# A decoder layer's running sums, kept token-major: the triangle of ones becomes the loaded operand, and the outputs are transposed instead of exp(-q)

## The reference, cut to what matters

```
qkv = _rms(x) @ w_qkv.T
q, k, v = jnp.split(qkv, 3, axis=-1)
q = _rms(q)
k = _rms(k)
w = jnp.exp(k)
kv_cum = jnp.cumsum(w * v, axis=1)
w_cum = jnp.cumsum(w, axis=1)
y = jax.nn.sigmoid(q) * (kv_cum / (w_cum + 1e-06))
uv = y @ w_swiglu.T
...
```

## Time and profile before

| | |
|---|---|
| median of three runs | 1407.77 us |
| the profiled execution | 1406.43 us |
| its span, first to last instruction | 1404.7 us |
| mean granted TensorE clock | 0.987 of full speed |
| TensorE busy with products over the span | 96% |
| VectorE, ScalarE, GpSimd busy | 58%, 43%, 37% |

### The profile page before, as it was taken

The page is one execution under the profiler, slowest core; times in us unless marked ns, Lnnn a source line. Parts: engine busy times, 40 slices in busy tenths (PEclk is TensorE's granted clock), DMA queues, the critical chain, the costliest instruction groups (busy, mean ns, idle before and its releaser), DMA issues.

```text
span 1404.7 us, 23677 instructions
## 1 busy us (share of the span) xinstructions
PE 1346.8 (96%) x8180; PEld 1072.4 (76%) x8180; DVE 819.7 (58%) x2085; ACT 607.9 (43%) x1135; POOL 515.2 (37%) x485
## 2 busy tenths in 40 slices
PE   8999999999999999999999999999988999999994
PEld 6788888888888888888877777777766887777662
DVE  5888765333333333333457787787776476666662
ACT  4444441111111111111127677777776223777772
POOL 4555442202020202020427654446453112565643
PEclk9999999999999999999999999999999899999997
DMA  6000012010010101010100000000011824465653
GB/s 255 1 0 0 0 42 94 0 45 26 21 45 1 45 0 45 0 46 0 49 27 2 20 21 20 21 20 3 5 47 59 351 86 157 85 110 93 106 97 45
DMA packets 20533, 73.41 MB, mean 52 GB/s; under 512 B 2320, under 2 KB 3344, under 8 KB 18000
## 3 DMA queue, kind: packets, MB, share of 16 engines
q0 software_dynamic: 10176, 25.17, 9.2%
q1 hardware_dynamic: 10256, 46.93, 9.0%
HBM read 52.95 MB, written 19.14 MB: 51 GB/s over the span
## 4 chain that ended last, share of the span: by engine, by line
PE 85%; DVE 6%; issue 3%; ACT 2%; DMA 2%; POOL 2%; DVEq 0%; POOLq 0%; ACTq 0%
PE ps L781 21%; PE ps L783 21%; PE ps L782 21%; PE ps L1029 6%; PE ps L1214 5%; PE ps L1021 2%; DVE den L1640 2%; PE ps L1053 2%; PE ps L1121 1%; PE ps L1018 1%; DMA h_rows<-hd 1%; PE ps L1047 1%; PE ps L1184 1%; POOL cols L673 1%; ACT cols L1434 1%
## 5 line engine op out<-in xcount | busy, mean ns | idle before, releaser
L781 PE MATMUL ps<-feat,wsplit 128*128 128x512 f32 (+1 forms) x672 | 247.2, 368 | 3.2 <-PE ps L783 2.2
L783 PE MATMUL ps<-feat,wsplit 128*128 128x512 f32 (+1 forms) x672 | 244.7, 364 | 0.0
L782 PE MATMUL ps<-feat,wsplit 128*128 128x512 f32 (+1 forms) x672 | 244.6, 364 | 0.0
L1291 ACT ACTIVATE sg<-ps 128x512 f32<-128x512 f32 x64 | 38.3, 598 | 368.8 <-PE ps L783 368.8
L1560 DVE TENSOR_TENSOR m_f<-ps,sg 128x512 f32<-128x512 f32 x64 | 44.2, 691 | 245.3 <-ACT sg L1291 245.3
L541 POOL CAST wsplit<-wraw 128x3072 fp32r<-128x3072 f32 x9 | 24.8, 2754 | 399.3 <-PEq L969 386.6
L1828 DVE CUSTOM_DVE_ANT_0 cols<-ps,msk 128x256 f32<-128x256 f32 (+1 forms) x512 | 146.1, 352 | 28.8 <-PE ps L1021 16.6
L781 PEld LDWEIGHTS ps<-feat,wsplit 128*128 128x128 f32 x672 | 126.7, 189 | 26.3 <-issue 6.6
L783 PEld LDWEIGHTS ps<-feat,wsplit 128*128 128x128 f32 x672 | 126.8, 189 | 20.1
L782 PEld LDWEIGHTS ps<-feat,wsplit 128*128 128x128 f32 x672 | 126.8, 189 | 19.6
L1422 ACT COPY cols<-ps 128x512 f32<-128x512 f32 x192 | 110.9, 578 | 61.2 <-PE ps L1029 61.2
(11 more groups left out here) (281 smaller groups left out, 3023.9 us busy)
## 6 DMA issues: line engine op xcount, KB each, us to landing
wraw<-weights SPq DMA_DIRECT2D x11, 1536.0 KB, 6.5
rawx<-weights SPq DMA_DIRECT2D x8, 1536.0 KB, 12.8
ctx_raw<-ctx_t SPq DMA_DIRECT2D x8, 512.0 KB, 4.6
h_rows<-hd POOLq DMA_DIRECT2D x16, 256.0 KB, 2.7
out<-acc SPq DMA_DIRECT2D x4, 1024.0 KB, 4.3
qkv_raw<-weights SPq DMA_DIRECT2D x6, 512.0 KB, 6.9
acc<-x SPq DMA_DIRECT2D x1, 3072.0 KB, 17.0
acc<-x SPq DMA_DIRECT2D x2, 512.0 KB, 6.8
```

The source lines that it names most:

```text
L781: nc.tensor.matmul(out_, w_hi, m_hi, start=first, stop=False)
L782: nc.tensor.matmul(out_, w_lo, m_hi, start=False, stop=False)
L783: return nc.tensor.matmul(out_, w_hi, m_lo, start=False, stop=last)
```

## The change

The two sides of the scan's products change places. `tri`'s two halves (triangle, and all ones) are now the loaded operand, and the data move through, 512 features at a time, tile by tile: tile 0 needs its own hi and lo for each of the two sums (4 products), tile 1 those of both tiles (8 products). The sums come out token-major, as `e_q` already lies, so exp(-q) is not transposed. ScalarE adds 1 to `e_q` in place (line 1329) and no longer copies w's sums; VectorE adds the 1e-6 where it added the 1. Tile t's output is transposed on TensorE (`turn_y`, lines 863 to 866) before its hi and lo go into `feat`, which are now read from PSUM. "Half 0" and "half 1" of the order become tile 0 and tile 1.

```diff
 (TensorE)
+            def scan(b, pb, tt):
+                if tt == 0:
                     pe.wait_ge(a["split"], 2 * b + 2)
-                    pe.wait_ge(a["e"], 2 * b + 2)
                 else:
-                    pe.wait_ge(a["y"], s)
+                    pe.wait_ge(a["y"], 2 * b + 1)
                 for bank, kind in ((5, 0), (4, 1)):
+                    terms = [(t, part) for t in range(tt + 1) for part in range(2)]
+                    for n, (t, part) in enumerate(terms):
+                        ones = tri[:, 0:P] if t == tt else tri[:, P:2 * P]
+                        mm = nc.tensor.matmul(ps[:, bank, :], ones, wv_s[:, place_a(pb, t), kind, part, :], start=(n == 0), stop=(n == len(terms) - 1))
+                mm.then_inc(a["scan"], 1)
+            def turn_y(b, tt):
+                pe.wait_ge(a["y"], 2 * b + tt + 1)
+                for k in range(KB):
+                    tr = nc.tensor.transpose(ps[:, 6, k * P:(k + 1) * P], den[:, k * P:(k + 1) * P], ident[:, :])
+                tr.then_inc(a["yT_ps"], 1)
...
                 project(b, 1, 0)
+                if not first:
+                    turn_y(b - 1, 0)
+                    scan(b - 1, 1 - pb, 1)
                 if not last:
                     transposes(b + 1, 0)
-                if not first:
-                    scan(b - 1, 1 - pb, 1)
                 project(b, 1, 1)
                 project(b, 1, 2)
+                if not first:
+                    turn_y(b - 1, 1)
...
 (ScalarE)
                 if tt == 1:
-                    after(act, a["scan"], 2 * b)
+                    after(act, a["den"], 2 * b)
...
+                act.wait_ge(a["e"], t + 1)
+                nc.scalar.activation(e_t, e_t, ACT.Copy, bias=1.0).then_inc(a["e1"], 1)
...
-                nc.scalar.activation(wce[:, :], ps[:, 5, :], ACT.Copy, bias=1e-6).then_inc(a["wce"], 1)
...
-                act.wait_ge(a["y"], 2 * b + half + 1)
+                act.wait_ge(a["yT_ps"], 2 * b + tt + 1)
...
 (VectorE)
-                dve.wait_ge(a["wce"], s + 1)
-                if half == 1:
-                    dve.wait_ge(a["yT"], s)
-                nc.vector.scalar_tensor_tensor(out=den[:, :], in0=ps[:, 6, :], scalar=1.0, in1=wce[:, :], op0=ALU.add,
+                dve.wait_ge(a["e1"], s + 1)
+                if tt == 1:
+                    dve.wait_ge(a["yT_ps"], s)
+                nc.vector.scalar_tensor_tensor(out=den[:, :], in0=ps[:, 5, :], scalar=1e-6, in1=e_q[:, place_a(pb, tt), :], op0=ALU.add,
...
-                nc.vector.tensor_tensor(feat[:, 1, 2 * half:2 * half + 2, cols], den[:, :].rearrange("p (k n) -> p k n", k=2),
+                nc.vector.tensor_tensor(feat[:, 1, :, cols], ps[:, 6, :].rearrange("p (k n) -> p k n", k=KB), feat[:, 0, :, cols],
```

More of the change, by code:

```diff
@@ L380, in decoder_layer @@
             w_hi_piece="pieces of w_qkv with hi", w_piece="pieces split", w2_hi="parts of the first MLP slot with hi", w2="parts split", shift="batches whose residual's scale and shift are made",
-            w_sum="running sums of w, half batches", scan="those of w * v and exp(-q)^T too", wce="w's sums plus 1e-6",
-            den="denominators", rec="their reciprocals", y="outputs, half batches", yhi="their hi in feat", yT="their lo too",
+            scan="tiles with the running sums of w and of w * v", e1="tiles of 1 + exp(-q)",
+            den="denominators", rec="their reciprocals", y="tiles of outputs", yT_ps="transposed in PSUM", yhi="their hi in feat", yT="their lo too",
             pool="GpSimd's own small steps", dve="the vector engine's")
@@ L454, in _ @@
             sp.wait_ge(a["split"], TILES)
-            sp.wait_ge(a["scan"], 2 * BATCH)
+            sp.wait_ge(a["den"], 2 * BATCH)
             sp.dma_start(wraw[:, 1, :], weights[3]).then_inc(raw_loaded[1], 16)
@@ L844, in project @@
                 mm.then_inc(a[name], 1)
-            def scan(b, pb, half):
-                s = 2 * b + half
-                if half == 0:
+            def scan(b, pb, tt):
+                if tt == 0:
                     pe.wait_ge(a["split"], 2 * b + 2)
-                    pe.wait_ge(a["e"], 2 * b + 2)
                 else:
-                    pe.wait_ge(a["y"], s)
-                at0, at1 = place_a(pb, 0), place_a(pb, 1)
+                    pe.wait_ge(a["y"], 2 * b + 1)
                 for bank, kind in ((5, 0), (4, 1)):
[L857 to L871, removed]
@@ L943, in run_mlp, with meanwhile @@
                 up, down = mlp_pe(pe, s_)
+                def meanwhile(j):
+                    if j == 1:
+                        turn_y(BATCH - 1, 1)
                 def steps(s0, count, slot_half, par_first, last, ch0=0):
@@ L959, in steps @@
                                     pe.wait_ge(a["yT"], 4 * (s + 2))
-                                up(s + 1, npar, nch, nch == 0, turn + 1, False)
+                                up(s + 1, npar, nch, nch == 0, turn + 1, False, meanwhile if isinstance(s, int) and s == 0 else None)
                                 if isinstance(s, int) and s == 0:
@@ L1317, in exp_q @@
                 if tt == 1:
-                    after(act, a["scan"], 2 * b)
-                squares(b, pb, tt, 0, e_q[:, place_a(pb, tt), :])
+                    after(act, a["den"], 2 * b)
+                e_t = e_q[:, place_a(pb, tt), :]
+                squares(b, pb, tt, 0, e_t)
                 if between:
@@ L1339, in wv_hi, with y_hi @@
                 nc.scalar.copy(wv_s[:, place_a(pb, tt), 1, 0, :], wv_f[:, :]).then_inc(a["wv_hi"], 1)
-            def w_cum(b, half):
-                s = 2 * b + half
-                act.wait_ge(a["w_sum"], s + 1)
-                nc.scalar.activation(wce[:, :], ps[:, 5, :], ACT.Copy, bias=1e-6).then_inc(a["wce"], 1)
-            def y_hi(b, half):
-                act.wait_ge(a["y"], 2 * b + half + 1)
-                cols = slice(b * SEQ, (b + 1) * SEQ) if isinstance(b, int) else bass.ds(b * SEQ, SEQ)
-                nc.scalar.copy(feat[:, 0, 2 * half:2 * half + 2, cols], den[:, :].rearrange("p (k n) -> p k n", k=2)).then_inc(a["yhi"], 1)
+            def y_hi(b, tt):
+                act.wait_ge(a["yT_ps"], 2 * b + tt + 1)
+                at_ = b * SEQ + tt * P
+                cols = slice(at_, at_ + P) if isinstance(b, int) else bass.ds(at_, P)
+                nc.scalar.copy(feat[:, 0, :, cols], ps[:, 6, :].rearrange("p (k n) -> p k n", k=KB)).then_inc(a["yhi"], 1)
             def batch_a(b, pb, first, last):
@@ L1354, in batch_a @@
                 hT_hi(b, 1)
-                exp_k(b, pb, 0, None if first else lambda: w_cum(b - 1, 0))
+                exp_k(b, pb, 0)
+                wv_hi(b, pb, 0)
                 if not first:
                     y_hi(b - 1, 0)
-                wv_hi(b, pb, 0)
                 if not last:
                     hT_hi(b + 1, 0)
[L1361 to L1366, removed]
+                exp_q(b, pb, 1, (lambda: first_hi(0)) if last else None)
                 exp_k(b, pb, 1, (lambda: first_hi(1)) if last else None)
@@ L1392, in _ @@
             first_hi(JB)
-            w_cum(BATCH - 1, 0)
-            y_hi(BATCH - 1, 0)
             step = mlp_act(act, mlp)
             step(0, 0, True)
-            w_cum(BATCH - 1, 1)
-            y_hi(BATCH - 1, 1)
+            for tt in range(TPB):
+                y_hi(BATCH - 1, tt)
             for s in range(1, 2 * CHUNKS):
@@ L1642, in y_a, with y_lo, batch_a @@
                 nc.vector.tensor_tensor(den[:, :], ps[:, 4, :], den[:, :], ALU.mult).then_inc(a["y"], 1)
-            def y_lo(b, half):
-                dve.wait_ge(a["yhi"], 2 * b + half + 1)
-                cols = slice(b * SEQ, (b + 1) * SEQ) if isinstance(b, int) else bass.ds(b * SEQ, SEQ)
-                nc.vector.tensor_tensor(feat[:, 1, 2 * half:2 * half + 2, cols], den[:, :].rearrange("p (k n) -> p k n", k=2),
-                                        feat[:, 0, 2 * half:2 * half + 2, cols], ALU.subtract).then_inc(a["yT"], 1)
-            def batch_a(b, first, last):
+            def y_lo(b, tt):
+                dve.wait_ge(a["yhi"], 2 * b + tt + 1)
+                at_ = b * SEQ + tt * P
+                cols = slice(at_, at_ + P) if isinstance(b, int) else bass.ds(at_, P)
+                nc.vector.tensor_tensor(feat[:, 1, :, cols], ps[:, 6, :].rearrange("p (k n) -> p k n", k=KB), feat[:, 0, :, cols],
+                                        ALU.subtract).then_inc(a["yT"], 1)
+            def batch_a(b, pb, first, last):
                 residual_a(b)
@@ L1768, in _ @@
             head, steps = mlp_dve(dve, mlp)
-            y_a(BATCH - 1, 0)
+            y_a(BATCH - 1, (BATCH - 1) % 2, 0)
+            head(0, 0)
             y_lo(BATCH - 1, 0)
-            head(0, 0)
-            y_a(BATCH - 1, 1)
+            y_a(BATCH - 1, (BATCH - 1) % 2, 1)
             y_lo(BATCH - 1, 1)
```

17 lines of the change are left out of this document (9 added, 8 removed).

## The result

The changed kernel takes 1419.43 us (median of 4 runs, 1419.03 to 1420.04), the kernel before beside it on the same chip 1408.12 (1401.96 to 1408.79): a ratio of 1.0091 [1.0062, 1.0119], slower by 11.3 us between the medians and 12.7 between the means. The profiled execution took 1420.04 us with a span of 1418.3, against 1406.43 and 1404.7 before: +13.6. Of the runs of the kernel before that stand beside the experiments, one of 2888.26 us, in a slower state, is left out of every comparison.

The account below looks back on a forecast made before the run. TensorE bounds the kernel before, with little to spare; the change closes a ring through all engines. On 1406.4 us, 13.5 for six passes plus 1.8 into the MLP give 1421.7, stated as 1422; range 1412 to 1429.

Parts of the forecast that it names:

- The ring: In stage A, the loop from den(b-1,1) through all engines to den(b,1) sets the pass: 24.57 to 25.27 us, taken as 24.92.
- The passes: Six stage A passes from T(1,1) to T(7,1), each 1.90 to 2.60 us longer: +13.5 in all (11.4 to 15.6).
- Into the MLP: Behind T(7,1): waits of 2.0, 1.2 and 0.7 us, less scan savings; together +1.8 (-2.1 to +3.9).
- y's lo part: VectorE's step in stage A reading PSUM: taken as 0.69 us; at 0.94, 0.25 more a pass, 1.5 in all.
- Costed at nothing: The second MLP slot's load waiting on SP for the last den, and ScalarE's y hi behind w*v's hi: nothing.
- A: Stage A: TensorE goes on deciding, a pass costs 20.8 us; total 1393, or 1398 with the old h wait; chance 0.07.
- two times from den to y: Case against TensorE deciding stage A: two den-to-y stretches, 8.2 us, counted in the loop's 14.1 of steps.
- B: Stage A: den does not hold back the square of q; only a shorter loop of 23.15 us remains; 1411; chance 0.12.
- C: Stage A: the loop holds and TensorE's clock falls too; 1428 us at 0.8 clock, 1424 at 0.91; chance 0.08.
- The signs by which it would show: Stage A: T(b,1) every 24.6 to 25.3 us, two idles of about 2 before transposes of den, TensorE 83% busy.

## Why the prediction was right

**The ring, link by link.** Sums from starts to starts, from den(4,1) to den(5,1), forecast against the blocks of rows above:

| links | forecast | measured |
|---|---|---|
| den to square of q | 0.81 | 0.71 |
| square of q, exponential, addition, to square of k | 3.65 | 3.61 |
| square of k to GpSimd's lo of w | 3.49 | 3.48 |
| lo of w, lo of w*v | 2.50 to 2.96 | 2.49 |
| GpSimd's steps to exponential | 1.48 to 1.72 | 1.73 |
| exponential, addition, hi, lo | 2.51 | 2.47 |
| den to y, y to turning | 4.86 | 4.84 |
| turning, scan, T(7,0), to hi | 2.88 | 3.05 |
| hi, lo, y's lo, h | 2.39 | 2.28 |
| ring | 24.57 to 25.27 | 24.66 |

No link is off by more than 0.17. Of the two that were left open, GpSimd's lo of w*v came out at the undisturbed end (1.25) and its steps at the upper one.

**The passes: +12.45, forecast 13.5.** T(1,1) to T(7,1) took 136.52 us before and 148.97 now. The ring was taken 0.25 too long (24.92 for 24.67, the middle where the lower end held), 1.5 in six passes. The first pass (25.15) and the fallen clock gave 0.9 of that back, and the forecast had neither. The pass before was taken from the last one as 22.67 where the six average 22.75, another 0.5. So the mechanism and the links are as forecast; that the sum came within 1 us is in part luck.

**Into the MLP: +1.0, forecast 1.8.** From T(7,1) to the first down product it was 43.09 us and is 44.06. The waits are where they were forecast, each smaller: 1.52 for y(6,0) (2.0), 0.85 for GpSimd's weight piece (1.2), 0.38 for y(7,1) (0.7). The first was taken over as "about 2 in every pass", though a pass's second wait is the longer one (1.75 against 1.51). With 13.5 and 1.8 as 12.45 and 1.0 the sum is 13.45, as the trace has it. One wait stood in no count: on the way to that product the kernel before waited for a step of VectorE's in the MLP, at 206.19, and the changed one does not.

```profile
PE ps L781 <- DVE m_f L1560: 0.6, 1, 0.6
```

**y's lo part** takes 0.68 to 0.69 every time, where it was 0.69 to 1.48: the value that was chosen, and what the Trainium skill, "SBUF — State Buffer", section "Who interferes with whom", has for one SBUF input.

**Costed at nothing, rightly:** the load that waits on SP for the last den (the first down product comes 13.47 later and the last instruction 13.6, so next to nothing is lost in between), and y's hi behind that of w*v. For y's hi the reason was wrong: it said that TensorE's turning comes later than w*v. In the rows above, turning ends at 171.05 and w*v at 172.22, so y's hi does wait, behind w*v's hi, until 172.78. It costs nothing only because ScalarE's next step, the hi of T(7,0), has to wait for T's end at 173.34 anyway. So the nothing was right by luck, and not for the reason that was given.

**The rivals.** A falls for the kernel as changed: TensorE does not decide. But one sentence of the case against it was wrong. It counted "two times from den to y" in the ring; the ring holds den to y once, in tile 0, and tile 1's steps hang beside it. The count should have been 10.0 us in place of 14.1, and since another order of the same instructions brings the pass down to TensorE's 20.98, the claim that "no two of its steps can run side by side" was an account of this order, not of the work. TensorE's 20.8 were a little low as well: the scan's products were put 0.2277 us apart, and eight of them take 1.93 (170.81 to 172.74), not 1.82. B was not this kernel, but the second place for exp(-q) made it, and its 23.15 measured 23.30. C happened once and cost 0.4 us: TensorE's clock fell to 1.2 GHz for some 3.5 us after the wait of 1.76 at 81.46 (0.57 granted from 82 to 86, the second row of the busy times above). That pass took 26.48, but the next only 23.29, with no wait before its first turning, at 96.36: together 49.77, where two rings are 49.34.

**The signs by which it would show.** These held: two waits in a pass before the transposes of `den` (one in the pass behind the fallen clock), released by VectorE's third step; the square of q in tile 1 waiting for den; y's lo; the rest of the kernel. These were off: the waits are 1.5 and 1.75 us, not about 2; TensorE is busy 87% (43.65 of 50), not 83%; scan products are 0.24 apart; one pass, of 24.48, is slightly under the 24.6 that was given, and two lie apart because of the fallen clock. One sign of being wrong did show, a granted clock under 1, but only in the stretch from 82 to 86 us.

## What to carry to other kernels

When an edit adds waits between in-order engines, add up the loop from a buffer's release back to its next release, start to start; where that sum is over the busiest engine's work per pass, it is the time, and what the busiest engine saves is lost. The links could be read from a trace of the kernel before to within 0.2 us, even for a loop that is not in it yet. Then move instructions out of the loop (into a stretch where the engine waits anyway, or behind the step that closes it) before giving up the edit: here two reorderings turned +0.9% into -0.6%.

## What was not expected of the hardware

The clock's fall was forecast as a danger in every pass, and waits of about 1.5 and 1.75 us came in every pass; yet only one stretch in six passes ran at the lower level in the profile of the changed kernel, one with the second place for exp(-q) (0.69 from 80 to 84 us) and one with the addition later (0.64 from 126 to 130), each behind a wait of 1.75 or 1.76. With T ahead of turning, where one wait of a pass is longer, there were four in six passes, behind waits of 3.04, 2.36, 2.52 and 2.44; behind those of 2.25 and 2.84 there was none. The second of them (the granted clock behind the engines):

```profile
97.00:101.00 4.00, 3.80 (x15) 3.38 (x16) 1.34 (x3) 1.69 (x3) 1.27 (x1) 0.59 0.00 0
```

What makes the difference between these waits and the others was not tried and stays open. From den to den such a stretch cost 0.4 us in the changed kernel and 1.8 with the second place for exp(-q). That fits the rings: the products behind the second wait, q(b+1,0), stand in the ring of rival B and not in that of the changed kernel. In the ten runs with the second place the longest (1420.32 us) had a mean granted clock of 0.982, the shortest (1408.79) 0.991. The kernel before shows the same link (1411.12 at 0.985, 1401.57 at 0.991), and these means go over the whole kernel, so they do not show that the time was lost in this stage.

Taking one SBUF input from y's lo part seems to have moved part of a contention (seen in the traces, not tried by itself). Means between 40 and 185 us, before and after: GpSimd's lo of w*v 1.50 and 1.29 us, VectorE's y's lo 1.05 and 0.69; but VectorE's addition of the residual, right behind y's lo, 0.78 and 0.92. In this order it lies outside the ring.
